# Moving the offset matmuls into the router's PSUM bank, the convolution into the other hat bank, and the ends of the instruction orders

## What is computed

```python
# tokenizer: 46 windows of K=16 positions, 64 channels
off = einsum('bwkc,ock->bow', xr, w_off) + b_off      # offsets dy, dx
px = base + dx;  wy = max(0, 1 - |dy|)
val = wy * linear interpolation of x at px             # by "hats"
h = einsum('bckw,dck->bwd', val, w_def) + b_def        # convolution
# attention on layernorm(h)
hid = tanh(hq[:, :, None] + hk[:, None] + b1); est = hid @ W2
h = h + softmax(QK/sqrt(d) + est) @ V
# experts on layernorm(h): router, 2 of 8 experts, a shared one
h = h + sum_e combine[e] * (relu(x @ w1[e] + b1[e]) @ w2[e] + b2[e]) + shared(x)
```

## Time and profile before

| | us |
|---|---|
| median of 3 runs | 1207.45 |
| lowest and highest | 1207.39, 1212.83 |
| the profiled execution, whole | 1209.83 |
| its span in the trace | 1208.0 |

### The profile page before, as it was taken

One profiled execution on the slowest core, in us unless ns is written; L12 is line 12 of the kernel. 1 busy time (PEld: TensorE's weight loads), 2 busy tenths in 40 slices (PEclk: granted clock), 3 DMA queues, 4 the chain that ended last, 5 costly groups with the idle time before them and its releaser, 6 DMA issues. The chain is left out here.

```text
span 1208.0 us, 16775 instructions
## 1 busy us (share of the span) xinstructions
PE 1071.2 (89%) x6214; PEld 501.0 (41%) x6214; DVE 683.1 (57%) x1293; ACT 913.7 (76%) x1431; POOL 2.0 (0%) x11
## 2 busy tenths in 40 slices
PE   3568798798989989898998989899898989989988
PEld 1234343444434444353444444344443434444544
DVE  2355546465654756566474656737465673756544
ACT  3596979696977969697796959879696986969343
POOL 0000000000000000000000000000000000000000
PEclk9799898999999999999999989999999999999989
DMA  7834343533544343354424334452443443230111
GB/s 255 248 111 159 109 154 104 169 108 109 183 141 165 102 165 115 108 168 158 165 97 154 129 108 166 145 177 86 152 147 108 166 139 125 92 138 4 61 63 65
DMA packets 63009, 160.56 MB, mean 133 GB/s; under 512 B 21456, under 2 KB 40144, under 8 KB 60624
## 3 DMA queue, kind: packets, MB, share of 16 engines
q1 hardware_dynamic: 62640, 159.18, 39.2%
q10 hardware_dynamic: 288, 0.32, 0.1%
HBM read 154.26 MB, written 5.21 MB: 132 GB/s over the span
## 5 line engine op out<-in xcount | busy, mean ns | idle before, releaser
L342 ACT ACTIVATE HT<-PXB,c_near 128x736 f32<-128x736 f32 x768 | 695.6, 977 | 63.8 <-PE bank L647 61.4
L647 PE MATMUL bank<-HT,XN 128*64 128x368 f32 x3072 | 537.7, 487 | 23.6 <-DVE HT L486 23.6
L486 DVE TENSOR_SCALAR HT<-HT 128x2208 f32<-128x2208 f32 x256 | 329.7, 1302 | 29.7 <-ACT HT L342 29.7
L647 PEld LDWEIGHTS bank<-HT,XN 128*64 128x64 f32 x3072 | 206.6, 138 | 307.1 <-issue 256.4
L611 PE MATMUL bank<-VT,c_mats 128*128 128x368 f32 x256 | 106.7, 583 | 62.7 <-DVE VT L496 62.7
L578 DVE TENSOR_TENSOR GE<-HE,CB 128x376 f32<-128x376 f32 x128 | 69.9, 548 | 154.4 <-ACT HE L411 144.1
L324 ACT ACTIVATE off<-bank,c_near 128x384 f32<-128x384 f32 x16 | 9.3, 581 | 153.5 <-issue 140.8
L759 PE MATMUL bank<-Z,c_experts 128*128 128x376 f32 x288 | 122.7, 509 | 0.0
L771 PE MATMUL bank<-GE,c_experts 128*128 128x376 f32 x256 | 110.5, 516 | 5.5 <-DVE GE L578 5.5
L611 PEld LDWEIGHTS bank<-VT,c_mats 128*128 128x128 f32 x256 | 59.2, 237 | 110.5 <-DVE VT L496 65.5
L411 ACT ACTIVATE HE<-bank,c_mats 128x376 f32<-128x376 f32 x128 | 72.4, 566 | 23.3 <-PE bank L759 22.8
(11 more groups left out here) (101 smaller groups left out, 678.3 us busy)
## 6 DMA issues: line engine op xcount, KB each, us to landing
PXB<-pw SPq DMA_DIRECT2D x64, 768.0 KB, 5.3
XT<-in_turned SPq DMA_DIRECT2D x16, 1536.0 KB, 9.3
XN<-in_x SPq DMA_DIRECT2D x64, 384.0 KB, 3.5
WYB<-pw SPq DMA_DIRECT2D x128, 192.0 KB, 5.5
CB<-shares SPq DMA_DIRECT2D x32, 752.0 KB, 4.0
out<-OUTS SPq DMA_DIRECT2D x16, 188.0 KB, 9.1
c_experts<-in_experts SPq DMA_DIRECT2D x1, 1152.0 KB, 20.3
c_mats<-in_mats SPq DMA_DIRECT2D x1, 1134.5 KB, 18.0
```

The source lines that it names most:

```text
L342: act.activation(HT[k % HTS][:, c, :, :].rearrange("p g (n w) -> p g n w", n=4), src, ACT.Abs, bias=cs["lneg"][:, 3 * half + c:3 * half + ...
L486: dve.tensor_scalar(rows_, rows_, 1.0, 0.0, ALU.subtract, ALU.min).then_inc(hat_ready, 1)
L647: mm = pe.matmul(bank[b % 2][64 * g:64 * g + 64, 0:2 * HW], XN[b // 2][:, b % 2, C * ch:C * ch + C], HT[k % HTS][:, c, 2 * g:2 * g + 2, :] ...
```

## The change

The offsets (`a3`, `a4`) go to bank 5, the router's. The convolution (`b3`) goes to bank 1. With this, hat `n0` of the next unit has bank 0 to itself and no longer waits for h0; hat `n2` does. The wait for the row positions moves from hat `n2` to `r7`, the next user of bank 5, and `a3` waits for the router of an earlier unit to have been read. The lists change at their ends and, in two places, at their starts.

```diff
--- before.py
+++ after.py
@@ -55,12 +55,12 @@
     "sync": {"d9": -3},
 }
 ORDER = {
-    "tensor": ("fs m1 n1 r7 f0 n2 r8 ds n3 d8 m2 n4 r9 f1 n5 m3 n6 r10 m4 n7 f2 n8 d0 m5 n9 m51 f3 n10 m52 d1 n11 r11 f4 "
-               "n12 d2 f5 n13 r12 d3 n14 f6 n15 d4 f7 d5 b3 a3 d6 a4 d7 m0 n0").split(),
+    "tensor": ("fs n1 m1 r7 f0 n2 r8 ds n3 d8 m2 n4 r9 f1 n5 m3 n6 r10 m4 n7 f2 n8 d0 m5 n9 m51 f3 n10 m52 d1 n11 r11 f4 "
+               "n12 d2 f5 n13 r12 d3 n14 f6 n15 d4 a3 f7 d5 a4 n0 b3 d6 d7 m0").split(),
     "scalar": ("k4 fs k5 r7 f0 k6 k7 k8 r9 f1 k9 m3 k10 m41 m4 k11 f2 k12 k13 m5 m51 f3 k14 m52 k15 f4 k0 f5 k1 r12 k2 f6 "
-               "k3 f7 a3 r6 a4 m0").split(),
-    "vector": ("r7 d8 j3 m1 o0 j4 r8 j5 m2 o1 j6 g0 g1 j7 m3 o2 j8 r10 m4 j9 o3 g2 j10 j11 o4 g3 j12 j13 r11 o5 g4 j14 j15 "
-               "g5 o6 r12 j0 r13 r14 g6 j1 r6 g7 j2 o7 b3 a4").split(),
+               "k3 a3 f7 a4 r6 m0").split(),
+    "vector": ("r7 d8 j3 o0 m1 j4 r8 j5 m2 o1 j6 g0 g1 j7 m3 o2 j8 r10 m4 j9 o3 g2 j10 j11 o4 g3 j12 j13 r11 o5 g4 j14 j15 "
+               "g5 o6 r12 j0 r13 r14 g6 o7 j1 a4 r6 g7 j2 b3").split(),
     "sync": ("d9 l0 l1 e0 e1 e2 l2 w0 p0 l3 x0").split(),
 }
 ORDERS = {
@@ -321,7 +321,7 @@
                 wait(act, ot_full, u)
                 act.wait_ge(off_full, u + 1)
                 wait(act, pw_out, 2 * 16 * u)
-                act.activation(off4[:, :], bank[1][:, 0:XCOLS], ACT.Identity, bias=cs["boff"][:, 0:1]).then_inc(off_ready, 1)
+                act.activation(off4[:, :], bank[5][:, 0:XCOLS], ACT.Identity, bias=cs["boff"][:, 0:1]).then_inc(off_ready, 1)
 
             def row_hats(m, h):
                 u = 2 * m + h
@@ -446,7 +446,7 @@
                 dve.wait_ge(ot_full, u + 1)
                 wait(dve, pw_out, 2 * 16 * u)
                 dve.tensor_tensor(rowx[:, :].rearrange("p (e c) -> p e c", c=RCOLS),
-                                  bank[1][:, 0:XCOLS].rearrange("p (e c) -> p e c", c=RCOLS),
+                                  bank[5][:, 0:XCOLS].rearrange("p (e c) -> p e c", c=RCOLS),
                                   cs["rowadd"][:, :].unsqueeze(1).broadcast_to([128, PAIRS, RCOLS]), ALU.add).then_inc(rowx_ready, 1)
 
             def rstd(ln):
@@ -500,7 +500,7 @@
             def b3(m, h):
 
                 dve.wait_ge(tok_full, 2 * m + h + 1)
-                dve.tensor_tensor(h0[h][:, :, 1:S], bank[0][:, 0:TOK].rearrange("p (b w) -> p b w", b=NB),
+                dve.tensor_tensor(h0[h][:, :, 1:S], bank[1][:, 0:TOK].rearrange("p (b w) -> p b w", b=NB),
                                   pe_b[:, 1:S].unsqueeze(1).broadcast_to([128, NB, W]), ALU.add).then_inc(h0_ready, 1)
 
             def m3(m, h):
@@ -608,26 +608,26 @@
                     pe.wait_ge(const_in, 16)
                 pe.wait_ge(dense_read, NB * (u + 1))
                 for q in range(KP):
-                    mm = pe.matmul(bank[0][:, 0:TOK], wdef[:, q, :], VT[:, q, :], start=(q == 0), stop=(q == KP - 1))
+                    mm = pe.matmul(bank[1][:, 0:TOK], wdef[:, q, :], VT[:, q, :], start=(q == 0), stop=(q == KP - 1))
                 mm.then_inc(tok_full, 1)
 
             def a3(m, h):
 
                 u = 2 * m + h
                 wait(pe, rowx_ready, u)
-                wait(pe, dense_read, NB * (u - 1))
+                wait(pe, lg_ready, u - 3)
                 pe.wait_ge(x_in, 16 * (u + 1))
                 for r in range(2):
                     for g in range(4):
                         q = 4 * r + g
-                        mm = pe.matmul(bank[1][32 * g:32 * g + 32, 0:XCOLS], wof[:, q, :], XT[:, q, :],
+                        mm = pe.matmul(bank[5][32 * g:32 * g + 32, 0:XCOLS], wof[:, q, :], XT[:, q, :],
                                        start=(r == 0), stop=(r == 1), skip_group_check=True)
                 mm.then_inc(off_full, 1)
 
             def a4(m, h):
 
                 pe.wait_ge(off_ready, 2 * m + h + 1)
-                pe.matmul(bank[1][:, 0:XCOLS], cs["selm"][:, :], off4[:, :], start=True, stop=True).then_inc(ot_full, 1)
+                pe.matmul(bank[5][:, 0:XCOLS], cs["selm"][:, :], off4[:, :], start=True, stop=True).then_inc(ot_full, 1)
 
             def dense(k):
                 def piece(m, h):
@@ -635,10 +635,8 @@
                     b, half = k // 2, k % 2
                     if half == 0:
                         wait(pe, dense_read, NB * u + b - 1)
-                        if b == 0:
+                        if b == 1:
                             wait(pe, h0_ready, u)
-                        if b == 1:
-                            pe.wait_ge(rowx_ready, min(u + 2, UNITS))
                         pe.wait_ge(xn_in[b // 2], 16 * (u + 1))
                     pe.wait_ge(hat_ready, HALVES * u + k + 1)
                     for c in range(CH // 2):
@@ -728,6 +726,7 @@
 
             def m7(m, h):
                 pe.wait_ge(p_ready, 2 * m + h + 1)
+                pe.wait_ge(rowx_ready, min(2 * m + h + 4, UNITS))
                 wait(pe, lg_ready, 2 * m + h)
                 pe.sem_inc(passed, 1)
                 for b in range(NB // 2):
```

## The result

The changed kernel takes 1143.45 us (median of 4 runs, 1142.9 to 1144.36), the kernel before 1208.7 (4 runs). The ratio is 0.9455, with a 95% interval of 0.943 to 0.948: 5.5% faster. The forecast was 1151, the range 1142 to 1168.

The account below looks back on a forecast made before the run. TensorE bounds the kernel, losing idle time and slow clock at period ends: 62.0 us, less new waits of 3.2 and 5.4, plus 4 at the first ends, gain 57.4; forecast 1151 us, range 1142 to 1168.

Parts of the forecast that it names:

- the clock term: Convolution at twelve period ends runs at a lower clock after TensorE's idle time: 17.1 us, 1.4% of the span.
- The steady gain: Twelve ends between 280 and 1080 us: 62.0 us of idle time and slow clock, less new waits, leaves 53.4 us.
- The wait at `a4`: TensorE waits for ScalarE's bias at the period end: a new 0.3 us, 3.2 us over eleven ends.
- The wait for PT: TensorE at `r8` waits 0.6 to 0.8 us instead of 0.24: 0.45 us more per period, 5.4 in twelve.
- The queue behind the squares: ScalarE's copies, two hats and relu from `m0` to `r8`: 8.0 to 8.2 us, where TensorE needs 7.4.
- The first ends: Three first period ends, where ScalarE leads because there are no experts yet: gains of 0.7, 1.7 and 1.7, 4 us together.
- the idle time at 151 us: An early period end: some 5 us of TensorE idle time stays, now ahead of `a4`; gain only 0.7 us.
- The moved waits: `r7` for row positions, `n2` for h0, `a3` for an earlier router: all ready well before wanted, costing nothing.
- The clock did not fall again: Rival: lower clock still granted at each period end, 17.1 us back, 1168; 12% together with missed new waits.
- ScalarE does not lead there: Rival that ScalarE leads everywhere: each steady end gives only 0.7 us, time 1197; 6%.
- the better case: Rival: `a4` and `r8` do not wait and the early ends gain in full, 1141 us; 10% for below 1145.
- The work put ahead of the convolution: TensorE runs offsets, expert matmuls and `n0` first at the period end; convolution starts at 642.7 without an idle gap.

Follow-up runs that it names:

- The filler: The kernel before, with five matmuls whose result nobody reads put ahead of each convolution from the fourth on: 1192.81 us, ratio 0.9857.

## Why the prediction was right, and where it fell short

**What bounds the kernel.** Right: idle time of TensorE at the period ends and the slow clock after it. The filler measured the clock term by itself, 16.5 us against 17.1.

**The steady gain.** The prediction booked 53.4 us for twelve periods, and 59.0 came. Two terms were mis-sized. The wait at `a4` was booked at 0.3 us per end, 3.2 in all (eleven times 0.3 is 3.3), and was 0.2 in all: the period end that I walked, at 642, is the one with the longest idle time of the twelve, 3.98 against 3.7 us, because ScalarE and with it VectorE came some 0.26 us later there (in the changed kernel the only wait at `a4`, 0.21 us, comes at this same end). The wait for PT was booked at 0.45 us more per period, and it was 0.3, from 0.25 to 0.56: the copies and the relu overlap more than the busy lengths say. The queue behind the squares was the right mechanism. The last microsecond is busy time: 18.1 us fell away where 17.1 were booked for the clock.

**The first ends.** Booked at 4 us. Up to the first steady `r8` 5.3 us came, 0.9 of which comes from constants that were there earlier (47.56 against 48.43). The clock fell at these ends while TensorE waited at `a4` (0.51 from 86 to 93 us), as foreseen. The prediction took the idle time at 151 us as one that the change leaves where it is; the runs with the early weighing show that the change itself kept it, by putting `a4` ahead of the convolution. Nothing was booked for the last convolution, whose wait of 1.1 us went too.

**The moved waits.** Right that they cost nothing: neither `r7` nor `n2` shows a wait in the steady stretch.

**The rivals.** The clock did not fall again at the steady ends (1.00). ScalarE does not lead there. What the walk called the better case lies at 1141, and the result came closer to it than to the forecast.

**What the prediction left out.** It took the change as a whole. The step "The weighing now follows the product of GE2: ... 4.2 us earlier. The convolution could start there" held the answer: by its own figures VT was ready at 637.9 and TensorE at about 638.0 in the old order. The work put ahead of the convolution was costed at nothing and counted as part of the cure. The runs show that it is no part of it: with the early weighing it adds 0.53 us per period, and 15.5 us by the medians (17 to 19 in the traces) at the first ends, where TensorE now stands at `a4` although VT is ready. By the medians, the change is a gain of about 84 us with a loss of 18 to 20 in it. The forecast held all the same, because the walk contained these losses (the waits at `a4` and `r8`, the idle time left at the first ends); it took them for the price of the gain, which they are not.

## What to carry to other kernels

When an engine waits for a piece, first ask what stands ahead of that piece in its producer's list. Moving one piece of 0.5 us was worth the whole gain here, and the new bank plan nothing. When a change has several edits, cost each against the others done: the second cure of the same wait was worth nothing here and brought a wait of its own. Work that is put ahead of a critical piece must depend on nothing later than that piece's own inputs, in the start-up phase too, where another engine may lead.

## What the runs showed of the hardware

Idle time of 3.7 us ahead of the convolution cost a second loss of 1.4 us in lower clock, on average: the granted clock fell at nine of twelve ends and stayed at 1.00 at three, behind idle time of the same length. TensorE work with no use, filled in, took that loss away (16.5 us of 1209). Shorter waits once per period left the granted clock at 1.00 throughout the steady stretch: 0.52 us at `a4` with the bias later, 0.6 at the convolution with the filler, 1.85 at the convolution with the weighing late.

The 1.1 MB of constants came at a different time in each run: SyncE issues them at 29.5 to 32.5 us in eleven of these traces, in the same order among the loads, and VectorE first uses them at 44.8 to 52.0 us. Issued by ScalarE at 14.8 us, they took 5.4 us from issue to landing, where it was 17.7 in the kernel without that edit. Everything up to the first period shifts with it, so small differences (under 5 us) between these kernels are safer read from the twelve periods than from the medians.
